# A two-layer mixture kernel: the second product turned round, with the activations held and the weight rows moving

## The reference

```
x = x + attn_a(layernorm(x))            # 16 heads of 16, causal softmax
x = x + ffn(layernorm(x), Wr, W1, b1, W2, b2)
x = x + attn_b(layernorm(x), ...)       # softmax over exp(-distance^2)
x = x + ffn(layernorm(x), Wr, W1, b1, W2, b2)
```

```
pooled = x.mean(axis=1);  logits = pooled @ Wr
top_scores, top_idx = top_k(logits, 2);  w = softmax(top_scores)
h = gelu(einsum('btd,bkdf->bktf', x, W1[top_idx]) + b1[top_idx])
y = einsum('bktf,bkfd->bktd', h, W2[top_idx]) + b2[top_idx]
out = einsum('bk,bktd->btd', w, y)
```

## Time and profile before

| what | value |
|---|---|
| median of 3 runs (all) | 1665.28 us (1665.22 to 1665.33) |
| profiled execution, its own time | 1663.65 us |
| its span, first to last instruction | 1661.9 us |
| mean granted TensorE clock | 0.999 |
| first mixture, about | 519 to 868 us |
| distance attention, about | 869 to 1308 us |
| second mixture, about | 1303 to 1662 us |

### The profile page before, as it was taken

The page is one execution under the profiler, slowest core; times in us unless marked ns, Lnnn a source line. Parts: engine busy times, 40 slices in busy tenths (PEclk is TensorE's granted clock), DMA queues, the critical chain, the costliest instruction groups (busy, mean ns, idle before and its releaser), DMA issues.

```text
span 1661.9 us, 27980 instructions
## 1 busy us (share of the span) xinstructions
PE 1615.9 (97%) x10531; PEld 755.2 (45%) x10531; DVE 1072.7 (65%) x2182; ACT 988.1 (59%) x1261; POOL 305.7 (18%) x402
## 2 busy tenths in 40 slices
PE   6999999999999999999999999999999899999998
PEld 2222222222233444444445666666666544444444
DVE  7533454354336865885557688868998886576554
ACT  6999999999997333533335555555445433353332
POOL 2012112112120000000005345544444200000000
PEclk9999999999999999999999999999999999999999
DMA  4012334100130003000000000000000200300000
GB/s 138 17 47 95 91 122 145 26 14 14 27 103 1 1 1 102 1 1 1 1 0 1 2 1 1 1 1 1 1 1 27 77 1 1 127 13 14 13 14 26
DMA packets 44338, 52.73 MB, mean 32 GB/s; under 512 B 3671, under 2 KB 39086, under 8 KB 44206
## 3 DMA queue, kind: packets, MB, share of 16 engines
q1 hardware_dynamic: 44206, 50.96, 9.8%
HBM read 38.88 MB, written 4.19 MB: 26 GB/s over the span
## 4 chain that ended last, share of the span: by engine, by line
PE 67%; ACT 16%; issue 10%; DVE 5%; POOL 1%; DMA 0%; ACTq 0%; DVEq 0%; SPq 0%; POOLq 0%
ACT a_probs L779 15%; PE f_h L1038 7%; PE f_ypsum L1039 7%; PE f_ypsum L1040 7%; PE f_ypsum L1038 7%; PE f_h L1039 7%; PE f_h L1040 7%; PE a_out L539 3%; PE d_outs L1038 3%; PE d_outs L1040 3%; PE d_outs L1039 3%; PE d_banks L1038 2%; PE d_banks L1039 2%; PE d_banks L1040 2%; PE a_scores L913 2%
## 5 line engine op out<-in xcount | busy, mean ns | idle before, releaser
L779 ACT ACTIVATE a_probs<-a_scores 128x1024 f32<-128x1024 f32 x544 | 499.9, 1210 | 6.6 <-PE a_scores L913 6.4
L1398 ACT ACTIVATE f_gelu<-f_h,f_bcol,s_more 128x512 f32<-128x512 f32 x256 | 199.1, 778 | 405.3 <-PE f_h L1040 393.8
L539 PE MATMUL a_out<-a_probs,a_values 128*32 128x512 f32 (+3 forms) x2560 | 293.3, 539 | 6.9 <-ACT a_probs L779 5.5
L1461 DVE TENSOR_SCALAR f_hh<-f_gelu,f_gates_scaled 128x512 f16<-128x512 f32 x256 | 125.0, 488 | 199.9 <-ACT f_gelu L1398 198.6
L1907 ACT ACTIVATE d_score<-d_dist,d_nksq,s_more 128x512 f32<-128x512 f32 x128 | 104.1, 814 | 191.1 <-DVE d_dist L2052 189.3
L1463 DVE SCALAR_TENSOR_TENSOR f_hl<-f_gelu,f_gates_scaled,f_hh 128x512 f16<-128x512 f32 x256 | 192.3, 751 | 9.1
L913 PE MATMUL a_scores<-a_moving,a_fixed 64*128 64x512 f16 (+3 forms) x1280 | 183.6, 353 | 9.7 <-ACT a_probs L779 3.7
L1944 POOL TENSOR_TENSOR distance_raw<-distance_raw,d_p 128x512 f32<-128x512 f32 x112 | 146.6, 1309 | 177.4 <-ACT d_p L1882 177.3
L793 POOL TENSOR_SCALAR_AFFINE_SELECT a_probs<-a_probs 128x256 f32<-128x256 f32 (+1 forms) x224 | 98.0, 453 | 419.5 <-ACT a_probs L779 417.7
L1038 PE MATMUL f_h<-c_xhi,f_w 128*128 128x512 f16 x384 | 145.6, 379 | 1.7 <-DVE f_w L1114 1.7
L1039 PE MATMUL f_h<-c_xlo,f_w 128*128 128x512 f16 x384 | 145.5, 379 | 0.0
(11 more groups left out here) (268 smaller groups left out, 2475.6 us busy)
## 6 DMA issues: line engine op xcount, KB each, us to landing
f_raw<-in_L_ffn_W SPq DMA_DIRECT2D x16, 1024.0 KB, 7.6
f_raw<-in_L_ffn_W SPq DMA_DIRECT2D x24, 512.0 KB, 8.1
a_fixed<-a_moving SPq DMA_DIRECT2D x60, 96.0 KB, 2.3
x<-in_L_attn_a_x SPq DMA_DIRECT2D x7, 512.0 KB, 6.3
out<-x SPq DMA_DIRECT2D x7, 512.0 KB, 2.9
f_raw<-in_L_ffn_W SPq DMA_DIRECT2D x12, 256.0 KB, 3.4
a_fixed<-a_moving SPq DMA_DIRECT2D x60, 32.0 KB, 2.0
f_early_raw<-in_L_ffn_W SPq DMA_DIRECT2D x4, 256.0 KB, 3.3
```

What stands on the lines that cost most here:

```text
L539: mm = pe.matmul(spare[32 * j:32 * j + 32, i % 2, skip:skip + w], values[:, G % 2, kt + tile, j, :], probs[:, u % UR, j % 2, col:col + w], ...
L779: act.activation(probs[:, u % UR], scores[:, 2 * (u % SR):2 * (u % SR) + 2, :], ACT.Exp, scale=HD ** -0.5)\
L1398: act.activation(gel[:, n % HR, :], hps[:, n % 2, :], ACT.Gelu, bias=mix.bcol[:, q, FT * e + j:FT * e + j + 1], scale=pr.scales.hidden)\
L1461: dve.tensor_scalar(hh[:, n % HR, :], gel[:, n % HR, :], gate, None, ALU.mult).then_inc(s_hh, 1)
```

## The change

The second product is turned round. In `down(n)` a 128-token piece of `f_hh` or `f_hl` is now held in the array, and a row block of W2 (128 hidden units by 256 output columns) moves: 4 token tiles x 3 matmuls of 256 columns in place of 2 x 3 of 512. The result has tokens on the partitions, as `x` has. A bank of `f_ypsum` holds two token tiles of 256 columns.

`result`, `turn_result`, the banks `f_misc` and the tile `f_y` are gone. `add_result` is one VectorE instruction for half a chunk, x = ypsum * scale + x, in steps 3 and 4. In the last chunk of the second mixture, its first half waits for the matmuls of tiles 0 and 1 alone.

The second bias now depends on the output column, which runs along the free side, so it is a row that all tokens share. `load_biases` loads the two rows of b2 into two partitions of `gathered`. `scale_b2` (VectorE, 3 instructions) multiplies each with its expert's weight, `widen_b2` (TensorE, one fp32 matmul with ones) sums them into all 128 partitions, `read_b2` (VectorE) copies that to `b2_wide`, and GpSimd adds `b2_wide` to each tile of `x`, once the tile has been normalised: 32 additions for each mixture, with `add_result` waiting for them (`s_xb`). These steps are made four times: once at the end of head attention, once at the end of distance attention, and once in each mixture for its second batch, in steps 49 to 51.

In distance attention the TensorE waits `banks_free` stand in the place of the two turns.

```diff
+        self.b2_rows = pr.gathered[0:TOPK, :]
+        self.own_gate = sb(f"{st}_own_gate", [TOPK, TOPK + 1], F32)
+        self.b2_wide = sb(f"{st}_b2_wide", [P, D], F32)
...
-            sp.dma_start(brow[o:o + KD, :], pr.b2[bass.ds(n, 1)].rearrange("o (k p) -> (o k) p", p=P)).then_inc(self.s_braw, 16)
+            sp.dma_start(self.b2_rows[e:e + 1, :], pr.b2[bass.ds(n, 1)]).then_inc(self.s_braw, 16)
...
+    def scale_b2(self, dve, q):
+
+        own = self.own_gate
         dve.wait_ge(self.s_gates, 2 * (q + 1))
...
+        dve.tensor_tensor(own[:, 0:TOPK], self.gate_cols[0:TOPK, q, :], self.pr.ident[0:TOPK, 0:TOPK], ALU.mult).then_inc(self.s_b2row, 1)
+        dve.wait_ge(self.s_b2row, 3 * q + 1)
+        dve.tensor_reduce(out=own[:, TOPK:TOPK + 1], in_=own[:, 0:TOPK], axis=AX.X, op=ALU.add).then_inc(self.s_b2row, 1)
+        dve.wait_ge(self.s_b2row, 3 * q + 2)
+        dve.wait_ge(self.s_braw, 4 * 16 * (q + 1))
+        dve.tensor_scalar(self.b2_rows, self.b2_rows, own[:, TOPK:TOPK + 1], None, ALU.mult).then_inc(self.s_b2row, 1)
+
+    def widen_b2(self, pe, q, bank):
+        pe.wait_ge(self.s_b2row, 3 * q + 3)
+        pe.matmul(bank[:, 0:D], self.pr.ones[0:TOPK, :], self.b2_rows, start=True, stop=True).then_inc(self.s_b2turn, 1)
+
+    def read_b2(self, dve, q, bank):
+        dve.wait_ge(self.s_b2turn, q + 1)
+        if q >= 1:
+            dve.wait_ge(self.s_xb, TILES * q)
+        dve.tensor_copy(self.b2_wide[:], bank[:, 0:D]).then_inc(self.s_b2w, 1)
...
                 if e == 0 and j == 0 and chunk >= 2:
-                    pe.wait_ge(s_y, KD * (chunk - 1))
+                    pe.wait_ge(s_added, 2 * (chunk - 1))
                 pe.wait_ge(s_hl, n + 1)
-                for k in range(KD):
-                    part, at = mix.parts[8 * e + 2 * (j // 2) + 1], slice(k * P, (k + 1) * P)
-                    mm = split_product(pe, yps[:, KD * (chunk % 2) + k, :], part[:, 0, j % 2, at], part[:, 1, j % 2, at],
-                                       hh[:, n % HR, :], hl[:, n % HR, :],
-                                       e == 0 and j == 0, e == TOPK - 1 and j == FT - 1)
-                    if last_layer and n == len(steps) - 1 and k == 0:
+                part = mix.parts[8 * e + 2 * (j // 2) + 1]
+                for t in range(TPC):
+
+                    tokens = slice(t * P, (t + 1) * P)
+                    mm = split_product(pe, yps[:, KD * (chunk % 2) + t // 2, (t % 2) * D:(t % 2 + 1) * D], hh[:, n % HR, tokens],
+                                       hl[:, n % HR, tokens], part[:, 0, j % 2, :], part[:, 1, j % 2, :],
+                                       e == 0 and j == 0 and t % 2 == 0, e == TOPK - 1 and j == FT - 1, shared=True)
+                    if last_layer and n == len(steps) - 1 and t == 1:
                         mm.then_inc(s_first_half, 1)
...
-            def add_result(chunk, half, bank=misc):
-                dve.wait_ge(s_rturned, chunk * (TPC // 2) + half + 1)
+            def add_result(chunk, half):
+                if last_layer and chunk == LAST and half == 0:
+                    dve.wait_ge(s_first_half, 1)
+                else:
+                    dve.wait_ge(s_used, (chunk + 1) * CS)
+                dve.wait_ge(mix.s_xb, chunk * TPC + 2 * half + 2)
                 xv = x[:, chunk * TPC + 2 * half:chunk * TPC + 2 * half + 2, :]
-                dve.tensor_tensor(xv, xv, bank[:].rearrange("p (t d) -> p t d", t=2), ALU.add).then_inc(s_added, 1)
+                dve.scalar_tensor_tensor(out=xv, in0=yps[:, KD * (chunk % 2) + half, :].rearrange("p (t d) -> p t d", t=2),
+                                         scalar=pr.scales.result, in1=xv, op0=ALU.mult, op1=ALU.add).then_inc(s_added, 1)
...
+            for tile in range(NB * TILES):
+                pool.wait_ge(cols.s_xn, 2 * base + tile + 1)
+                if tile % TILES == 0:
+                    pool.wait_ge(mix.s_b2w, tile // TILES + 1)
+                pool.tensor_tensor(x[:, tile, :], x[:, tile, :], mix.b2_wide[:], ALU.add).then_inc(mix.s_xb, 1)
+
+        def banks_free(pe, which):
+
+            pe.wait_ge(s_added, (TPC // 2) * (LAST + which))
...
-              122: [("spread",)],
-              123: [("weights", 3)],
-              124: [("turn_biases",)]}
+              122: [("spread",), ("gates",)],
+              123: [("weights", 3), ("turn_biases",)],
+              124: [("biases",), ("scale_b2",)],
+              125: [("widen_b2",)],
+              126: [("read_b2",)]}
...
+            banks_free(pe, 0)
             project(0, 0)
-            finish_ahead(pe, 0)
             project(0, 1)
-            finish_ahead(pe, 1)
+            banks_free(pe, 1)
             project(1, 0)
```

More of the change, by code:

```diff
@@ L848, in last_group @@
                     reads[0].append((mix.s_bcol, 1))
+                elif at == 34:
+                    free(0)
+                    mix.widen_b2(pe, 0, spare[:, 0, :])
+                    reads[0].append((mix.s_b2w, 1))
             def turn(job, tiles=range(TPC)):
@@ L1314, in do @@
                     mix.turn_biases(pe, what, side)
+                elif kind == "widen_b2":
+                    side_free(mix.s_b2w, what + 1)
+                    mix.widen_b2(pe, what, side)
             def up(n):
```

126 lines of the change are left out of this document (39 added, 87 removed).

## The result

The changed kernel takes 1653.18 us, the median of four runs (1652.26 to 1654.33), against 1665.25 us for the kernel before in the same job (1663.81 to 1665.33). The ratio is 0.993, with a 95% interval of 0.9913 to 0.9947. The forecast was 1654.3 us in a range of 1651 to 1659, so the time lies in the range and the sign is the one forecast. The two medians are 12.1 us apart, where the forecast had 11.0.

What follows compares the result with a forecast made beforehand. The prediction took TensorE's issue time to bound the mixtures. Its terms, -12.8 + 3.8 + 1.1 + 0.1 - 1.9 + 0.8 - 2.1 = -11.0 us, took 1665.28 to 1654.3 us, range 1651 to 1659.

Steps and rivals of the forecast that it cites:

- Turns: Inside the mixtures: 28 turns of four fp32 transposes removed at 0.44 us each, 0.5 for four others: -12.8 us.
- The sum: Whole kernel: all priced terms added together, -11.0 us, giving a forecast of 1654.3 us.
- Smaller matmuls: In the mixtures' `down`: 12 matmuls of 256 columns for 6 of 512, 0.015 us more a step: +3.8 us.
- The rival of weight loads that show: In the mixtures: late weight loads delay all 3072 small matmuls; 16 us slower at 10 ns over; chance 0.05.
- The second bias in the mixtures: Two widening matmuls on TensorE's path inside the mixtures, 0.55 us each: +1.1 us (0.6 to 1.3).
- At the end of head attention: Widening matmul issued there, where ScalarE's exponentials and GpSimd's masks end last: 0 to 0.6, taken as +0.1 us.
- GpSimd's additions: 64 additions of 0.75 us, a pair costing VectorE about 0.4 us, covered by its idle time: 0.
- From the mixture to distance attention: Projections no longer stopped by turns, norms begin 3.3 us sooner, first scores gain 1.4 to 2.3: -1.9 us.
- The end of distance attention: Widening before step 126's scores waits for `scale_b2`, TensorE 3.5 us late, most of it regained: +0.8 us (0 to 3).
- 1.95 of the 3.5 come back: End of distance attention: of 3.5 us lateness, TensorE regains 1.95 from idle time between 1292.48 and 1299.63.
- The first rival: End of distance attention: VectorE, locked beside GpSimd, is the bound; loss near 5 us, not 0.8: 1658.5; chance 0.09.
- The end: End of program: no `f_y` or turn before the last additions, which end at 1655.45, not 1657.58: -2.1 us.

Runs made afterwards that it cites:

- Experiment 2: The kernel before, with every turn of the second product's result made twice into the same bank: 1677.32 us, ratio 1.0081.
- experiment 1: The kernel before, with each 512-column matmul of the second product cut into two of 256, W2 still held: 1667.11 us, ratio 1.002.
- experiment 4: The changed kernel without any work on the second bias (scaling, widening, copy and additions left out): 1649.64 us, ratio 0.9911.
- 9: The changed kernel with GpSimd's last ten sums of distance attention cut from 512 columns to one, result incomplete: 1649.12 us, ratio 0.9911.
- experiment 7: The changed kernel with distance attention's last tasks later: biases turned at step 124, second bias scaled at 125, widened at 127, read at 128: 1652.81 us.
- experiment 5: The changed kernel with distance attention's widen_b2 and read_b2 two steps later, at 127 and 128: 1651.73 us, ratio 0.9925.
- experiment 3: The changed kernel without GpSimd's 64 additions of the bias row (second bias missing from the result): 1654.21 us, ratio 0.9937.

## Why the prediction was right

**Turns.** The sum had 28 at 0.44 us and 0.5 for the other four. Experiment 2 has 0.436 for each of the 28. In a mixture of the changed kernel 3.73 us are gone; with 1.83 for small matmuls (experiment 1) and 0.73 for the widening (experiment 4) given back, the turns were worth 3.73 + 1.83 + 0.73 = 6.29, or 12.6 in both, against the 12.3 of the sum. Experiment 2 doubles the turns without their waits for `f_y`, and so has 12.2.

**Smaller matmuls.** The sum had 0.015 us a step, from the pitch in distance attention; the steps went from 2.590 to 2.605. The rival of weight loads that show is out: the tile's row gives the loads of the new form as 97 to 98 ns, each under a pitch of 109.

```profile
L1044 PEld LDWEIGHTS f_ypsum<-f_w,f_hh x768: 97/98/98, 539.8 to 1646.7; 128*128 128x128 f16 x192
```

By the Trainium skill ("TensorE: Matmul & The Clock Gate", What overlaps and what doesn't) such loads would not overlap, as they fill all rows of the array. The trace disagrees: the changed kernel's 3072 small matmuls follow each other 2822 times directly, always at 0.108 to 0.110 us. The measurement decides.

**The second bias in the mixtures** was mis-sized: 1.46 us for the two, where the sum had 1.1 and a range up to 1.3. I took 0.55 for one widening, next to a row of its kind at 0.63; 0.72 is right. The 0.63 of the earlier trace rows would have been nearer (657.41 to 658.04 has the same 0.63), with 0.09 ahead of it that no row of before shows. That the total fits all the same is luck: the turns gave 0.3 more than I had. At the end of head attention the sum had +0.1, and the table has +0.14; without any bias work 0.44 us go there (experiment 4).

**GpSimd's additions** cost nothing, for the reason that the prediction gave: VectorE's idle time of 1.3 us in a step takes up 0.4. Thirty of 256 `f_hh` were held up, to 0.86 to 0.95 us, two of them by the additions of `bvo` as before.
**From the mixture to distance attention** came out at 2.3 with the two turns, against 2.15. TensorE starts the projections at 866.93 and doesn't stop in them. VectorE's timeline has its two additions at once, and the norms at 868.46, 1.5 us behind the start of the projections, where it was 4.8 us (868.71 to 873.52 in the earlier trace rows); the sum had 3.3 us for this step too.

```profile
867.13 1.41 DVE L1440 SCALAR_TENSOR_TENSOR x<-f_ypsum,s_more,x 128x512 f32<-128x512 f32 x2 [3.15 <-PE f_ypsum L1046]
868.46 0.72 DVE L1015 TENSOR_SCALAR c_xn<-x,mv,rstd 128x256 f32<-128x256 f32 x2
```

**The end of distance attention** came out at the +0.8 of the sum, but in part for another reason than I gave, so the number is luck here. I had one wait, of about 3 us, ahead of the widening. There are two, and the first, 1.49 us for the gates, stands at a place that I hadn't priced: the turn of the biases, which the change moved up by a step. "1.95 of the 3.5 come back" holds in kind, since all five gaps of before are gone. What I missed is what sets the pace: GpSimd's sums, beside which VectorE's instructions take 1.44 and 1.54 us in place of 0.37 and 0.75. I saw it in one row (1.28 us for 128x2 elements) and used it as a delay of one instruction. The first rival had the mechanism, VectorE held up by GpSimd as the bound of the stretch, but at a price near 5 us. That hold-up is there in the kernel before as well, and what the change adds to it is the 0.8. Experiments 4 and 9 show what is left: 1.9 us of that stretch go without the second bias, 3.4 with the sums short. A further 0.4 us came back where TensorE waits for the weights of mixture 2, which the sum had at nothing; that wait moves by as much between kernels that don't touch it, so this isn't shown to be the change's.

**The end** gave 2.1 us, as the sum had it. The quarter of a microsecond that I had put down for two turns besides is not there: the turns were part of that chain already.

What stays open: whether and how often the granted clock falls behind the two new waits (one of the two profiles that have them both), what moves the wait for the weights of mixture 2, and what in the last steps of distance attention the order of tasks moves, as experiment 7 ends 1.1 us above experiment 5 with fewer waits for new work (0.4 of it in that stretch, 0.9 in the wait for the weights).

## What to carry to other kernels

Where the timeline shows one engine issuing without a gap, price a change by pitches from the same trace, term by term; here each such term held to 0.4 us. Exchange the sides of a product when that lets the result come out as the next step needs it: the price is that of the smaller moving side, 0.015 us for a step of 12 such matmuls, and not that of more weight loads. Where an engine waits for short instructions of VectorE, look at what GpSimd runs beside them before you move tasks about: two moves gained 0.8 us and lost 0.4, short sums gained 3.2. Those sums left part of the result out, so this says what lighter work on GpSimd could be worth, not how to get it. And a row that all partitions need can come by DMA, if its factors are a column of scalars: that is worth 2.0 us here, at 128 KB to load for a row.

## What the runs showed that I had not expected

In the profiles, the two groups of times go with the granted clock at the start. These are windows of the changed kernel's profile and of that of the kernel before, columns as in the earlier trace rows:

```profile
20.00:25.00 5.00, 3.06 (x44) 1.20 (x38) 4.53 (x13) 3.79 (x5) 3.52 (x7) 0.93 0.02 5
25.00:30.00 5.00, 5.00 (x44) 1.53 (x36) 2.41 (x7) 2.60 (x3) 0.00 (x0) 0.73 0.37 94
```
```profile
20.00:25.00 5.00, 3.44 (x50) 1.31 (x44) 4.54 (x12) 3.97 (x5) 3.48 (x7) 1.00 0.02 5
25.00:30.00 5.00, 4.99 (x54) 1.61 (x50) 3.72 (x16) 4.40 (x5) 0.00 (x0) 1.00 0.39 73
```

In four of the twelve profiles the clock is 0.73 to 0.81 at 25 to 30 us, and in these four `a_out<-bvo,ones` starts at 493.6 to 493.8; in the other eight it is 1.00, and the row stands at 491.8 to 492.2. What the two windows lose by it, 7% and 27% of 5 us in the first fence, is 1.7 us, and it is 1.7 in each of the four. Ahead of the fall TensorE sat idle for 1.94 us in these four profiles, and for 0.95 to 1.56 us at the same place in the other eight. In the changed kernel's profile it is this row, in that of before it has 1.56 us up to 23.45:

```profile
23.66 0.61 PE L867 MATMUL a_scores<-ident,a_split_m 128*128 128x128 f16 x8 [1.94 <-DVE a_split_m L603]
```

The exception is experiment 3: its profile starts with a clock of 1.00, and the fall at 1290 us puts it in the upper group. The other runs have no trace, so for them the cause is inferred; nor is it shown why the idle time differs. So the span that the profile of the changed kernel shows, 9.5 us less, has 1.8 us in it that aren't the change's. Whoever compares single profiles of such kernels has to look at the clock by windows first.
